# Mamba mixer: one mask instruction for four groups of heads, over a ring of three fours

## The reference, cut to what matters

```
def step(hst, inp):
    dA_t, dBx_t, B_t, C_t = inp
    hst = hst * dA_t[:, :, None, None] + dBx_t[..., None] * B_t[:, None, None, :]
    y = jnp.einsum('bhpn,bn->bhp', hst, C_t)
    return (hst, y)
...
y = ssd_scan(xh, dt, Bm, Cm, A)
y = y + D_skip[None, None, :, None] * xh
y = y * jax.nn.silu(z)
y = y * jax.lax.rsqrt(jnp.mean(jnp.square(y), axis=-1, keepdims=True) + 1e-05) * rms_w
return y @ out_proj_w
```

## Time and profile before

| | us |
|---|---|
| median of three runs (2952.26 to 2956.80) | 2955.95 |
| the profiled execution: its time | 2960.77 |
| the profiled execution: its span | 2959.1 |
| PE busy (share of the span) | 2753.9 (93%) |
| DVE busy | 1786.3 (60%) |
| ACT busy | 1394.1 (47%) |
| POOL busy | 637.6 (22%) |

### The profile page before, as it was taken

One profiled execution on the slowest core, in us unless ns is written; L12 is line 12 of the kernel. 1 busy time (PEld: TensorE's weight loads), 2 busy tenths in 40 slices (PEclk: granted clock), 3 DMA queues, 4 the chain that ended last, 5 costly groups with the idle time before them and its releaser, 6 DMA issues. The chain is left out here.

```text
span 2959.1 us, 46148 instructions
## 1 busy us (share of the span) xinstructions
PE 2753.9 (93%) x17002; PEld 2071.6 (70%) x17002; DVE 1786.3 (60%) x3230; ACT 1394.1 (47%) x2405; POOL 637.6 (22%) x718
## 2 busy tenths in 40 slices
PE   4899999999999897999999999999999999999999
PEld 2455555555555554888887878878787877878787
DVE  6898999999999986677764333233333323333332
ACT  3877777777777774566553222222222222222221
POOL 4122222222222223000001222222222212222221
PEclk7899999999999999999999999999999999999999
DMA  2111010101010110532221000000000000000000
GB/s 66 33 44 37 22 38 29 38 23 38 22 38 22 38 38 31 169 139 66 69 66 31 15 17 15 1 17 15 17 15 17 15 1 17 15 17 15 17 15 8
DMA packets 103993, 99.46 MB, mean 34 GB/s; under 512 B 35800, under 2 KB 98520, under 8 KB 103008
## 3 DMA queue, kind: packets, MB, share of 16 engines
q1 hardware_dynamic: 102176, 96.36, 10.5%
q10 hardware_dynamic: 1600, 0.04, 0.0%
HBM read 68.00 MB, written 37.80 MB: 36 GB/s over the span
## 5 line engine op out<-in xcount | busy, mean ns | idle before, releaser
L1706 PE MATMUL fbank<-hid,fw 128*128 128x512 f32 x4096 | 962.3, 395 | 0.0
L1706 PEld LDWEIGHTS fbank<-hid,fw 128*128 128x128 f32 x4096 | 765.4, 187 | 187.7
L1849 DVE TENSOR_TENSOR hid<-fhf,hid 128x512 fp32r<-128x512 f32 x384 | 264.7, 689 | 703.9 <-POOL hid L1809 703.9
L1809 POOL TENSOR_SCALAR hid<-fhf 128x512 fp32r<-128x512 f32 x384 | 269.3, 701 | 1070.8 <-ACT fhf L1783 762.3
L1212 DVE SCALAR_TENSOR_TENSOR mh<-mh,gm 128x1024 f32<-128x1024 f32 x256 | 353.6, 1387 | 0.0
L918 ACT ACTIVATE mh<-ebank 128x512 f32<-128x512 f32 x512 | 294.2, 596 | 104.4 <-PE ebank L765 102.0
L1783 ACT ACTIVATE fhf<-fbank,sh2c 128x512 f32<-128x512 f32 x128 | 88.0, 687 | 382.6 <-PE fbank L1706 382.6
L765 PE MATMUL ebank<-cright,cleft 102*128 102x512 bf16 x512 | 210.6, 412 | 58.6 <-ACT mh L918 53.5
L778 PE MATMUL yin<-mh,xpad 128*32 128x128 f32 x4096 | 228.1, 297 | 30.3 <-DVE mh L1212 30.3
L752 PE MATMUL ebank<-ah,win 128*128 128x512 f32 x640 | 247.7, 430 | 5.2 <-ACT cin L951 5.2
L1783 ACT ACTIVATE fhf<-fbank,sh1c 128x512 f32<-128x512 f32 x128 | 87.9, 687 | 320.9 <-PE fbank L1706 320.7
(11 more groups left out here) (194 smaller groups left out, 4295.5 us busy)
## 6 DMA issues: line engine op xcount, KB each, us to landing
tok<-in_x SPq DMA_DIRECT2D x24, 512.0 KB, 4.9
tok<-x_d SPq DMA_DIRECT2D x17, 512.0 KB, 3.9
h_d<-in_h SPq DMA_DIRECT2D x16, 512.0 KB, 5.2
o_d<-tok SPq DMA_DIRECT2D x16, 512.0 KB, 2.9
fw<-h_d SPq DMA_DIRECT2D x2, 4096.0 KB, 15.3
out_x<-tok SPq DMA_DIRECT2D x16, 512.0 KB, 3.3
tok<-o_d SPq DMA_DIRECT2D x8, 512.0 KB, 3.9
mx<-in_x SPq DMA_DIRECT2D x8, 512.0 KB, 4.7
```

The lines of the kernel that those rows point to most:

```text
L1706: mm = pe.matmul(bank[banks.slot(key)][:], w[:, k, m * P:(m + 1) * P].bitcast(dt), h[:, k, :].bitcast(dt), start=(k + n == 0), stop=(k == ...
L1809: pool.tensor_scalar(hid[i % 2][0][:, m, :], hf[j % 3][:], 1.0, 0.0, ALU.mult, ALU.add)\
L1849: dve.tensor_tensor(hid[i % 2][1][:, m, :], hf[j % 3][:], hid[i % 2][0][:, m, :].bitcast(F32), ALU.subtract).then_inc(c_lo.sem, 1)
```

## The change

`masked` runs at every fourth step in place of every second, and takes groups i-3 to i in one instruction of 2048 columns. The ring `mh` holds three fours (12 groups, 24 KB of each partition) in place of four pairs (8 groups, 16 KB). PE's `intra` and ACT's `exponent` wait for and release fours. The semaphore waits of `masked` become four in place of two, `addends` waits for the second four of its chunk. `LAG` and all tables of steps stay.

```diff
-MH = 8
+MH = 12
+MG = 4
...
-    h_mh = Handover(sem, "mh", [(q, i) for q in chunks for i in range(NG // 2)], MH // 2, uses=2)
+    h_mh = Handover(sem, "mh", [(q, i) for q in chunks for i in range(NG // MG)], MH // MG, uses=MG)
...
-    mh = [sb(f"mh{j}", [P, 2, G4, P]) for j in range(MH // 2)]
+    mh = [sb(f"mh{j}", [P, MG, G4, P]) for j in range(MH // MG)]
...
             def intra(q, i):
-                key = (q, i // 2)
+                key = (q, i // MG)
...
             def masked(q, i):
-                key = (q, i // 2)
-                if i == 1:
+                key = (q, i // MG)
+                if i == MG - 1:
                     released(dve, ("bt", q))
-                released(dve, ("eb", q, i - 1))
-                released(dve, ("eb", q, i))
+                for one in range(i - MG + 1, i + 1):
+                    released(dve, ("eb", q, one))
...
-                                         in1=gm[q % 2][:].unsqueeze(1).to_broadcast([P, 2 * G4, P]),
+                                         in1=gm[q % 2][:].unsqueeze(1).to_broadcast([P, MG * G4, P]),
...
             def addends(q):
-                last = (q, NG // 2 - 1)
+                last = (q, NG // MG - 1)
...
-                if i % 2 and has_chunk(q):
+                if i % MG == MG - 1 and has_chunk(q):
                     masked(q, i)
```

More of the change, by code:

```diff
@@ L779, in intra @@
                                    xpad[q % 2][:, G4 * (i // 2) + j, i % 2, :, :].rearrange("s w d -> s (w d)"),
-                                   mh[h_mh.slot(key)][:, i % 2, j, :], start=(i % 2 == 0), stop=(i % 2 == 1),
+                                   mh[h_mh.slot(key)][:, i % MG, j, :], start=(i % 2 == 0), stop=(i % 2 == 1),
                                    tile_position=(0, row))
@@ L915, in exponent @@
                 made(act, key)
-                pair = (q, i // 2)
-                act.wait_ge(h_mh.free(pair), h_mh.used_before(0, pair))
-                nc.scalar.activation(mh[h_mh.slot(pair)][:, i % 2].rearrange("s h t -> s (h t)"), tile(key)[:],
+                some = (q, i // MG)
+                act.wait_ge(h_mh.free(some), h_mh.used_before(0, some))
+                nc.scalar.activation(mh[h_mh.slot(some)][:, i % MG].rearrange("s h t -> s (h t)"), tile(key)[:],
                                      ACT.Exp).then_inc(free(key), 1)
```

## The result

The changed kernel takes 3433.3 us (3429.2 to 3436.0), against 2954.7 us for the kernel before in the same comparison: a ratio of 1.162, 95% interval 1.160 to 1.164. It is slower, as forecast, and for the greater part by the mechanism forecast, but 83 us more than the 3350 us predicted, and 3 us outside the range.

A forecast was written before the change was run, and what follows sets the result against it. In the mixer's 1070 us PE and DVE were both taken to be near their limit, over 90% busy. Profiled 2961 + 275 (loop) + 14 (late addends) + 103 (clock) = 3353, so about 3350 us; range 3245 to 3430, 8 in 10.

The forecast's parts named there:

- The closed loop: At each turn of chunks PE's first product waits for a mask behind addends that wait for PE's last product: +275 us.
- the late addends: In some turns DVE reaches the addends under 1 us late: between 0 and 30 us, taken as 14.
- the second mask of the chunk: DVE's mask at i = 7, needed for PE's i = 10: about 10 us available, 4 to 8 taken, so no wait.
- the clock's: In the mixer, three new falls to half clock a block, 45 of 5.7 us at 0.4: +103 us, bounds 0 and 175.
- the clock would hold: Rival for PE's clock in the mixer: it holds or falls seldom, 3235 to 3290 us; 12 in 100.
- it would stay down for most of the mixer: Rival for PE's clock: low for 0.6 of the mixer's 1360 us, costing 290 us, 3540 us in all; 8 in 100.
- DVE's saving counted at 0: 128 fewer mask instructions save DVE 8 to 18 us, but DVE will have time to spare, so 0 at the end.
- The ring of three fours: The wider mask ring takes away a wait of ACT's exponentials that was never met: 0 us.

The follow-up runs named there:

- e3: The changed kernel with DVE's weights (dend, wv) one step later, behind the mask of groups 4 to 7: 3351.6 us, 1.133.
- e7: The kernel before, with pairs, and only the addends two steps earlier, ahead of the mask that PE's next product needs: 3284.9 us, 1.111.
- e9: The changed kernel with both masks of 2048 columns one step earlier in DVE's order, ahead of the addends and of `dend`: 3026.2 us, 1.022.
- e4: The changed kernel with PE's decay product ahead of each of the five stalls repeated 14 times into the same bank: 3360.4 us, 1.136.
- e2: The changed kernel with each mask of 2048 columns issued as two of 1024 in the same place, released together: 3456.7 us, 1.169.

## Why the prediction was wrong in its size

*The closed loop* was right in mechanism and nearly in size: 289 us with the late addends, less what PE waited elsewhere, against 332.9 - 30.3 = 303 us in e3, which has the turns alone. Idle time at each turn of the changed kernel: n = 6 took 4.9 us (4.9 in the prediction), n = 30 3.6 (3.6), n = 14 6.5 (5.5), n = 22 5.8 (5.2, from which the 0.66 us of waiting that stood there before are already taken). At n = 14 the difference is for the greater part DVE coming 0.7 us late for the addends, for which I had allowed under 1 us. e7 shows the loop without fours, e9 its going when the order is turned round.

*The step that failed* is the sentence that the second mask of the chunk would bring no wait: DVE has "the whole of PE's steps 6 to 9 for it, about 10 us, and takes 4 to 8". The 4 to 8 us were durations from a trace in which DVE's masks started 2 to 10 us behind ACT's exponentials, so that no wait for ACT was in them. In the loop DVE is close behind PE, and `dend` at n = 14 waits for ACT's n = 16. That is the fifth stall, 57.5 us of idle and the clock's falls behind it. e3 takes it out alone: 82 us, and the kernel then takes 3352 us, where the prediction said 3350. So the miss of 83 us is this term, by what its removal wins.

That the rest agrees to 2 us is partly luck. In e3 the waits for masks are 14 us above the terms for them, the other waits of PE went down by about 15 us, for which the sum had nothing, and in *the clock's* term two errors met. PE's busy time rose by 104 us in e3 (2857.7 against 2753.9) and by 130 in the changed kernel, against 103 predicted. I counted 45 new falls of 5.7 us, 257 us more at the low level. The trace of e3 has 47 more stretches at the low level than the kernel before (63 against 16), so the count was right, but they are longer: 512 us against 96 in all. And I took 0.4 us for each microsecond, from the lengths of single products, where e4 gives 0.25 and the busy time 104 / 416 = 0.25. Why a microsecond costs less than the products' lengths say is not shown by any run. e4 shows that the term is real: 73 us come back for extra work on PE. The rivals that the clock would hold, and that it would stay down for most of the mixer, were both wrong (0.81).

*DVE's saving counted at 0*: right. DVE's busy time fell by 12.6 us (1786.3 to 1773.7), inside the 8 to 18 us reckoned, and DVE waited more instead. The masks' group fell by 39 us, but that counts time in which a mask and its neighbour run at once. e2 shows the fixed part where it does stand in the path, 0.13 us a turn.

*The ring of three fours*: ACT's exponentials wait only for PE's decay, as before. No experiment varied the ring alone; e9 keeps it and is 71 us above the kernel before, which leaves little for the ring to cost there.

The Trainium skill, "TensorE: Matmul & The Clock Gate" (Why this matters for your kernels), says that idle gaps between bursts put the engine back to half rate: behind each of PE's 79 waits for a mask of 3.4 us or more in the changed kernel the granted clock was 0.50 (before 16 of them it was down already). The Trainium skill, "VectorE: DVE Perf Modes" (The TRN2 errata), says that a large tile pays the fixed latency once: this held for the instruction, 2.29 us in place of 2 x 1.22, and the kernel was 478 us slower all the same.

What stays open: which part of e9's 71 us a better table of steps could win back, and what the ring costs by itself.

## What to carry to other kernels

A coarser unit moves a handover later by the width of the unit, and in a hand-written order it may jump over a wait: before merging instructions, look for one between the old places that waits for the engine that will wait for the merged one. Place the merged instruction by what stands ahead of it, not by its last input. And when an engine loses its lag, its durations from the old trace are short by all the waits that the lag had hidden: read the two engines' tables of steps against each other for every place where one asks for a later step of the other.

## What the runs showed of the hardware

More work made the kernel faster: 13 extra products of 512 columns at each stall brought the granted clock in the mixer from 0.81 to 0.90 and the time down by 73 us (e4). Behind a stall of 3.13 us the product of 0.43 us still took 0.66.

Which of DVE and POOL starts first decides who pays. With the mask 0.37 us ahead, POOL's instruction of 512 columns took 3.19 us and the mask 0.15 us more than alone (changed kernel); with POOL ahead, a mask of 1024 columns took 2.28 us in place of 1.22, and POOL's instruction 2.13 us (e2).
